# Two layers of a gated Flamingo-style network on one core: transposed q and k projections in the self attention, a later output product in the first cross attention, and phase ends without a second wait

## What is computed

```
x = x + tanh(g_xattn[0]) * _L0_xattn_ref(_layernorm(x), ctx_2048, ...)   # 16 heads of 128, keys 64 per sequence
x = x + tanh(g_ffn[0])  * _L0_ffn_ref(_layernorm(x), ...)                # self attention, then mixture of experts

q = (h @ wq + bq).reshape(b, s, H, HD).transpose(0, 2, 1, 3)             # H = 16, HD = 128
k = (h @ wk + bk) ...;  v = (h @ wv + bv) ...
q = q * cos + _rotate_half(q) * sin
k = k * cos + _rotate_half(k) * sin                                      # _rotate_half: (-x2, x1) of the halves of a head
probs = softmax(q k^T / sqrt(HD), causal);  out = (probs @ v) @ wo + bo
```

## Time and profile before

| | |
|---|---|
| median of 3 runs | 2107.55 us (2107.46 to 2110.78) |
| profiled execution: its time, its span | 2106.73 us, 2104.8 us |
| PE / PEld / DVE / ACT / POOL busy | 88% / 77% / 52% / 58% / 47% of the span |
| mean granted PE clock | 0.937 |
| x0, f0 in the trace | about 95 to 394 us, 448.6 to 1112 us |

### The profile page before, as it was taken

The page is one execution under the profiler, slowest core; times in us unless marked ns, Lnnn a source line. Parts: engine busy times, 40 slices in busy tenths (PEclk is TensorE's granted clock), DMA queues, the critical chain, the costliest instruction groups (busy, mean ns, idle before and its releaser), DMA issues.

```text
span 2104.8 us, 36109 instructions
## 1 busy us (share of the span) xinstructions
PE 1850.6 (88%) x11456; PEld 1614.3 (77%) x11456; DVE 1100.6 (52%) x3059; ACT 1228.7 (58%) x4061; POOL 979.7 (47%) x1133
## 2 busy tenths in 40 slices
PE   3599999449999999999997897489999999999698
PEld 1377887327888888888887785278888888988598
DVE  1467666555565565565552443455555555555422
ACT  1266777225666666666662331388888888888321
POOL 2333333276775775775543101254444444444255
PEclk9699999659999999999995898699999999999799
DMA  3000000100000000000000101000000000000000
GB/s 102 23 13 16 16 21 26 48 29 31 11 31 16 12 31 16 11 16 16 11 11 1 33 25 38 22 7 11 10 8 11 11 11 11 18 18 12 4 16 26
DMA packets 29069, 42.26 MB, mean 20 GB/s; under 512 B 4690, under 2 KB 18514, under 8 KB 28628
## 3 DMA queue, kind: packets, MB, share of 16 engines
q1 hardware_dynamic: 28884, 39.96, 6.3%
HBM read 35.76 MB, written 4.19 MB: 19 GB/s over the span
## 4 chain that ended last, share of the span: by engine, by line
PE 65%; ACT 13%; issue 6%; DVE 5%; POOL 3%; PEld 1%; DMA 1%; POOLq 1%; SPq 0%; PEldq 0%; DVEq 0%; ACTq 0%
PE pA L460 6%; PE pA L462 6%; PE pA L461 6%; PE pS L894 4%; PE pF L460 3%; ACT pA L1444 3%; PE pF L461 3%; PE pF L462 3%; PE pF L626 3%; PE pO L913 3%; PE pS L605 3%; PE pT L886 2%; ACT x_P L1470 2%; PE pT L903 2%; PE pO L1363 1%
## 5 line engine op out<-in xcount | busy, mean ns | idle before, releaser
L460 PE MATMUL pA<-Wh,XTh 128*128 128x512 f32 (+1 forms) x768 | 345.8, 450 | 21.9 <-POOLq L120 12.1
L462 PE MATMUL pA<-Wh,XTl 128*128 128x512 f32 (+1 forms) x768 | 292.9, 381 | 0.0
L461 PE MATMUL pA<-Wl,XTh 128*128 128x512 f32 (+1 forms) x768 | 292.0, 380 | 0.0
L455 POOL TENSOR_TENSOR Wl<-RAW,Wh 128x512 fp32r<-128x512 f32 (+3 forms) x96 | 102.1, 1063 | 402.0 <-ACT Wh L448 402.0
L460 PEld LDWEIGHTS pA<-Wh,XTh 128*128 128x128 f32 x768 | 148.6, 193 | 51.3 <-POOLq L120 13.3
L1192 POOL TENSOR_TENSOR f_t<-f_t,f_RB 128x512 f32<-128x512 f32 x128 | 165.3, 1291 | 16.9 <-DVE f_t L1076 16.7
L462 PEld LDWEIGHTS pA<-Wh,XTl 128*128 128x128 f32 x768 | 148.0, 193 | 28.8
L461 PEld LDWEIGHTS pA<-Wl,XTh 128*128 128x128 f32 x768 | 148.8, 194 | 26.6
L1076 DVE TENSOR_TENSOR f_t<-pA,f_sin 128x512 f32<-128x512 f32 x128 | 88.5, 692 | 140.7 <-PE pA L462 99.9
L1470 ACT ACTIVATE x_P<-x_P,x_nm 128x192 f32<-128x192 f32 (+1 forms) x256 | 127.3, 501 | 32.6 <-DVE x_nm L1579 32.5
L1002 ACT ACTIVATE f_P<-f_P,f_nm 128x128 f32<-128x128 f32 (+1 forms) x256 | 113.6, 447 | 49.7 <-DVE f_nm L1095 49.4
(11 more groups left out here) (247 smaller groups left out, 5873.1 us busy)
## 6 DMA issues: line engine op xcount, KB each, us to landing
RAW<-in_w_f SPq DMA_DIRECT2D x32, 256.0 KB, 2.6
RAW<-in_w_x SPq DMA_DIRECT2D x32, 160.0 KB, 2.2
RAW<-in_w_x SPq DMA_DIRECT2D x32, 128.0 KB, 2.0
RAW<-in_w_ff SPq DMA_DIRECT2D x8, 288.0 KB, 2.8
R<-in_x SPq DMA_DIRECT2D x4, 512.0 KB, 5.9
x_spill<-R SPq DMA_DIRECT2D x1, 2048.0 KB, 7.5
f_bqk<-in_f_b SPq DMA_DIRECT2D x4, 512.0 KB, 3.7
RAW<-in_w_moe SPq DMA_DIRECT2D x8, 256.0 KB, 2.7
```

The costliest lines, as they stand in the source:

```text
L455: pool.tensor_tensor(Wl[slot][:, at], RAW[:, s, 0:cw], Wh[slot][:, at].bitcast(F32), ALU.subtract).then_inc(split_done, 1)
L460: e.matmul(o, ah, bh, start=first, stop=False)
L461: e.matmul(o, ah, bl, start=False, stop=False)
L462: return e.matmul(o, al, bh, start=False, stop=last)
```

## The change

It has three parts.

**Phase ends.** All engines wait for `bar`; `cleared` is gone. POOL clears the old phase's semaphores behind that wait, while the others go on. The semaphores of a phase are given back one phase later than before, so neighbouring phases use different ones.

**x0.** `out_proj(i - 1)` stands behind `p_tr(i)` in PE's order, and the last one behind the loop. PT and VW get a second copy each; DVE's `add_out` follows one step later, inside the softmax.

**f0.** q and k are projected transposed: weights stationary, 256 tokens moving, twelve matrix multiplications of 128x256 for each n (two heads, two k tiles, three products). The parts are now n = 0: q of heads 0 and 1, n = 1: k of heads 0 and 1, n = 2 and 3 the same for heads 2 and 3. Since a head's features lie on partitions, its halves are swapped by ACT, `swapped`: two copies of 64x512 from pA to the other half of `sw`, which has two buffers. DVE `take` writes (pA + bias) x cos straight to qT or kT, two operations of 128x256. POOL `rotate` has three operations of 128x512: sw x sin, + RB, and the sum. `qk_tr` and `qk_ev` are gone. RB is made by ACT (`swapped_bias`, two operations of 128x256 in 12 of the steps and four times ahead of them). `w_high` and `w_low` are both on DVE. qT and kT get a second copy.

```
         def phase_end(e, name):
             k = phases.setdefault(name, len(phases) + 1)
             e.drain().then_inc(bar, 1)
+            e.wait_ge(bar, 5 * k)
             if e is nc.gpsimd:
-                e.wait_ge(bar, 5 * k)
                 for h in sems_of[name]:
                     e.sem_clear(h)
-                e.nop().then_inc(cleared, 1)
-            e.wait_ge(cleared, k)
...
                     p_tr(i)
-                    out_proj(i, s)
+                    if not first:
+                        out_proj(i - 1, 1 - s)
                 in_order(e, NI, body, 24)
+                out_proj(NI - 1, (NI - 1) % 2)
...
+                    if i >= 2:
+                        add_out(i - 2)
                     if two_more:
                         queries(i + 2, s, 0)
...
-                    for k in range(KD):
-                        cc = slice(w0 + k * GW, w0 + (k + 1) * GW)
-                        ins = three(e, pA[:, n % 2, :], x_part(XTh, i, k, t), x_part(XTl, i, k, t),
-                                    Wh[g % 2][:, cc], Wl[g % 2][:, cc], k == 0, k == KD - 1)
+                    for a in range(2):
+                        o = pA[:, n % 2, a * S:(a + 1) * S]
+                        h = 2 * (n // 2) + a
+                        for k in range(KD):
+                            at = WK * (n % 2) + k * GW + h * HD
+                            w = slice(at, at + HD)
+                            xh, xl = XTh[:, k, b], XTl[:, k, b]
+                            e.matmul(o, Wh[g % 2][:, w], xh, start=(k == 0), stop=False)
+                            e.matmul(o, Wh[g % 2][:, w], xl, start=False, stop=False)
+                            ins = e.matmul(o, Wl[g % 2][:, w], xh, start=False, stop=(k == KD - 1))
...
+                def swapped(i, n):
+                    m = NT * i + n
+                    e.wait_ge(q["proj"], NQ * i + n + 1)
+                    e.wait_ge(q["rope"], pos(m - 1))
+                    for r in range(2):
+                        src, dst = slice(r * H2, (r + 1) * H2), slice((1 - r) * H2, (2 - r) * H2)
+                        ins = e.activation(sw[dst, n % 2, :, :], pA[src, n % 2, :].rearrange("p (a n) -> p a n", a=2),
+                                           ACT.Copy)
+                    ins.then_inc(q["sw"], 1)
...
                     if n < 4:
+                        e.wait_ge(q["sw"], NT * i + n + 1)
+                        e.wait_ge(q["sc"], pos(HG * (i - 1)))
+                        x = (kT if n % 2 else qT)[:, i % 2, 2 * (n // 2):2 * (n // 2) + 2, :]
+                        for a in range(2):
+                            h = (i // 8) * HG + 2 * (n // 2) + a
+                            ins = e.scalar_tensor_tensor(x[:, a, :], pA[:, n % 2, a * S:(a + 1) * S],
+                                                         bqk[:, n % 2, h:h + 1], cosd[:, :], ALU.add, ALU.mult)
+                        ins.then_inc(q["taken"], 1)
...
                 def rotate(i, n):
                     m, g = NT * i + n, i // 8
+                    y = sw[:, n % 2, :, :]
+                    x = (kT if n % 2 else qT)[:, i % 2, 2 * (n // 2):2 * (n // 2) + 2, :]
+                    e.wait_ge(q["sw"], m + 1)
+                    e.tensor_tensor(y, y, bc(sind[:, :], 1, 2), ALU.mult).then_inc(q["swm"], 1)
+                    e.wait_ge(q["swm"], m + 1)
+                    e.wait_ge(q["rb"], 2 * NT * g + 2 * n + 2)
+                    e.tensor_tensor(y, y, RB[:, g % 2, 2 * n:2 * n + 2, :], ALU.add).then_inc(q["swb"], 1)
+                    e.wait_ge(q["swb"], m + 1)
                     e.wait_ge(q["taken"], NQ * i + n + 1)
                     e.tensor_tensor(x, x, y, ALU.add).then_inc(q["rope"], 1)
```

More of the change, by code:

```diff
@@ L774, in body @@
                     if last:
+                        add_out(i - 1)
                         add_out(i)
@@ L880, in qk_tr @@
[L880 to L888 removed]
+                    if n >= 4:
+                        for k in range(KD):
+                            cc = slice(WV + k * GW, WV + (k + 1) * GW)
+                            ins = three(e, pA[:, n % 2, :], x_part(XTh, i, k, n - 4), x_part(XTl, i, k, n - 4),
+                                        Wh[g % 2][:, cc], Wl[g % 2][:, cc], k == 0, k == KD - 1)
+                        ins.then_inc(q["proj"], 1)
+                        return
@@ L931, in pe @@
                     proj(0, n)
-                for n in range(NT):
-                    qk_tr(0, n)
                 proj(1, 0)
@@ L1016, in o_ev @@
                     e.activation(OTh[:, i % 2, h, :], pO[:, 0:S], ACT.Copy).then_inc(q["oth"], 1)
-                def w_high(i):
-                    g = i // 8
-                    e.wait_ge(q["proj"], NQ * 8 * g)
-                    e.wait_ge(q["f"], pos(i - 1))
-                    high_w(e, raw_in, q["hi"], cw_next if g == G - 1 else cw_here, i, i % 2, (g + 1) % 2)
+                e.wait_ge(q["const"], 64)
                 for n in range(NT):
-                    qk_ev(0, n)
+                    swapped_bias(0, n)
+                    swapped(0, n)
+                swapped(1, 0)
                 exp(0, 0)
+                swapped(1, 1)
                 normalise(0, 0)
+                swapped(1, 2)
                 exp(0, 1)
                 for i in range(NI):
-                    j = i + 1
-                    one = j < NI
+                    j, k = i + 1, i + 2
+                    one, two = j < NI, k < NI
                     p_ev(i, 0)
+                    if one:
+                        swapped(j, 3)
                     normalise(i, 1)
@@ L1142, in dve @@
                     recip(i, 3)
+                    w_high(i)
                     o_low(i, 1)
+                    w_low(i)
                     if i:
                         add_out(i - 1)
+                    if one:
+                        soft(j, 0)
                     if two:
@@ L1149, in dve @@
                     if one:
-                        soft(j, 0)
-                    if two:
-                        take(k, 1)
-                    if one:
                         recip(j, 0)
```

225 lines of the change are left out of this document (75 added, 150 removed).

## The result

The changed kernel takes 2048.65 us (median of 4 runs, 2046.52 to 2050.59), the kernel before in the same series 2109.16 (2107.46 to 2111.98). The ratio is 0.9712, with a 95% interval of 0.9695 to 0.9728: 60.5 us less, where 2057 us and 50.0 us less than the profiled run were forecast. The profiled execution has a span of 2046.1 us.

A forecast was written before the change was run, and what follows sets the result against it. PE was taken to bound f0, and after the change a loop through sw's two buffers. Gains 14.3 + 17.8 + 9.4 + 0.9 + 6.1 + 1.5 = 50.0 us off 2106.73 gave 2057 us; eight-in-ten range 2038 to 2088.

The forecast's parts named there:

- Phase ends: At all phase ends, 210 semaphore clears leave the path and 0.6 us come back in layer norms: 14.3 us gained.
- x0: First cross attention: PE's 0.69 us wait for the PT copy goes in 30 steps, less the last step's cost: 17.8 us.
- the likeliest case: The forecast itself, with an f0 period of 19.4 to 19.8 us and its unknown prices: chance 0.56, 2048 to 2068 us.
- The tail: End of x0: the last step pays for one more output product and addition, taken as 2.9 us lost.
- f0, what PE saves: Each f0 step loses 1.95 us of transposes, new projections cost nothing; PE alone would need 17.86 us a step.
- f0, the loop: Loop through sw's two buffers, rotations 0 and 1 and proj(k,5): period 19.6 us instead of 19.81, 6.1 us gained.
- The sign named beforehand: In f0, PE idle 1.5 to 1.8 us before each proj(·,5), released by DVE; a PE wait elsewhere would be wrong.
- f0, its start: f0 starts 9.4 us earlier, with small constants; first period gives 0.9 more, the stretch behind proj(31,5) 1.5.
- The unbound loop: Rival, chance 0.10: f0's loop does not bind, PE never waits before proj(k,5); period 17.9, 2008 us.
- ScalarE was not late: Rival, chance 0.17: ACT's swaps in f0 wait behind exp or softmax copies; period 20.0 to 20.6, 2069 to 2086 us.
- The collision of GpSimd and VectorE: Rival, chance 0.10: w_high and w_low on DVE hold up rotations 0 and 1; period 20.6 or 21.0, 2086 or 2098 us.
- The other rule that was weighed: Following copies overlap by about 93 ns: f0's loop 0.19 us shorter, sum 5.4 us lower; the forecast did not use it.

The follow-up runs named there:

- four buffers: The changed kernel with four buffers of sw instead of two, so the swap of n = 3 waits only for the step before's rotation: 2015.73 us, ratio 0.9552.
- both GpSimd experiments: The changed kernel with one more 128x512 GpSimd operation in rotations n = 0 and 1: 2168.77 us; or in n = 2 and 3: 2053.99 us.
- the split on the other engines: The changed kernel with the weights' high part back on ScalarE and low part on GpSimd, in places beside the loop: 2049.85 us, ratio 0.972.

## Why the prediction was right or wrong

The range and the direction were right, and so was the mechanism of f0. The time lies 8.4 us under the forecast value, at the lower edge of the likeliest case's own range (2048 to 2068). Against the 50.0 us of the forecast the traces differ by 58.7: 7.5 more in x0 and 3.2 more in f0's periods, 2.0 less in the rest.

- **Phase ends**: 14.3 forecast, 13.6 measured alone. That the clears lie beside other work except ahead of two norms was confirmed by clearing twice.
- **x0**: 17.8 forecast, 26.4 measured alone. This is the term that was mis-sized. It was "30 x 0.69 = 20.7 us", with the price taken from the idle time of the earlier trace rows; the runs show 0.90 to 0.93 a step, 28.1 us. The tail, 2.9, is 2.8 in the trace (28.1 less the 25.3 to the last addition). The surplus is outside the bound that the prediction gave this term (2 us more), and inside the range of the sum only because that was wide enough for it. The wait was gone as forecast; its price has to be read from start to start.
- **f0, what PE saves**: "PE alone would need 17.86 us": 17.87 with four buffers, when the two gaps that are left are taken out. The new projections cost nothing, as said. Of the 1.95 us that the transposes took, 0.3 was a wait: at 772.74 the four of KR start 0.74 us behind the four of QR, at 768.06 only 0.44. That wait went with them, so the sum holds. From `proj(j,5)` to the end of `proj(k,0)` it is 7.87 us instead of the 7.98 forecast.
- **f0, the loop**: 19.63 us forecast and 19.6 taken, 19.49 measured. Every link was found where it was put: swap 1.19 (1.21), two rotations 7.98 from 711.29 to 719.27 (8.04), swap 1.19, take 0.88. The four buffers and both GpSimd experiments show that it is this loop. The sign named beforehand, 1.5 to 1.8 us of idle PE before `proj(·,5)` and no wait elsewhere, came out only in part: 1.07 is printed, 1.31 from start to start, and 0.31 stands ahead of `proj(k,3)`. 29 periods gave 9.3 us instead of 6.1, since 0.1 us counts 29 times.
- **f0, its start**: 9.4 forecast, 8.7; first period 0.9 and 0.3; behind the last projection 1.5 and 2.4. In all 11.8 forecast, 11.4 measured.
- **The rivals.** The unbound loop would have needed more buffers. ScalarE was not late for the loop with two buffers (its swap of n = 1 kept `proj(k,3)` back by 0.31 us, beside the loop), but it is what remains with four. The collision of GpSimd and VectorE occurs, in the changed kernel at the other end: not POOL's rotations but DVE's copy is held up. The timeline and the view of that line show it:

```profile
706.56 1.42 DVE L1098 CAST Wh<-RAW 128x512 fp32r<-128x512 f32 x1
```
```profile
L1098 DVE CAST Wh<-RAW x32: 426/1419/1496, 455.4 to 1050.6; 128x512 fp32r<-128x512 f32 x32
```
```profile
706.40 1.28 POOL L1170 TENSOR_TENSOR f_kT<-f_kT,f_sw 128x512 f32<-128x512 f32 x1
```

The copy takes 0.43 us at least and 1.42 in the median, and here it ends 0.30 us after the POOL operation that began ahead of it. POOL's 384 operations of f0 stay between 1.26 and 1.30 us. It goes both ways, though, where the timing differs: with the operation added in n = 2 and 3, DVE's copy and the subtraction behind it (711.90 to 714.88) run beside the two POOL operations of 1.47 and 1.61 us shown above. By the rule in the Trainium skill, "SBUF — State Buffer", section "SBUF: two separate sides", who comes first keeps the shared port for a whole instruction and the other waits; the trace agrees. Its price for the loop was nothing, as the kernel with the split on the other engines shows. The other rule that was weighed, "ScalarE: Activation LUTs", section "What ACT_TABLE_LOAD costs" in the Trainium skill, would have made a swap pair 0.09 us shorter than two singles: the trace disagrees within a pair, with 1.19 us for two of 0.593. It agrees with the rule for what follows: the normalising behind the swap of 719.37 starts at 720.47, 0.09 before that swap ends, which shortens nothing in the loop.

What stays open: why the second cross attention starts later than in the kernel before, by 1.4 us in the changed kernel and by 0.6 to 3.2 in the kernels with one part alone. The trace of the changed kernel shows one DMA issue of 1.48 us ahead of it instead of 0.43, in a stretch in which the instruction queue has a packet that the kernel before lacks. That alone is not the cause: with the phase ends alone no issue there is long, and the start comes 2.0 us later all the same.

## What to carry to other kernels

Price a wait on TensorE by the distance between starts, with and without it, not by the idle time that a view prints: here 0.93 against 0.69 us, and gaps of 0.3 us with no idle time at all. When a change takes work off the bounding engine, look for the loop through buffers that it leaves, and add up its links; two buffers in such a loop can give back nearly all that was saved (of 1.95 us a step off TensorE, 1.62 came back as waiting). Where several engines work in strict order around a single buffer, moving one operation ahead moves the wait to the buffer's other reader; reorder all who share it, or add a buffer.

## What was not expected of the hardware

- A loop that leaves TensorE waiting can lose clock on top. In the kernel with an added operation in n = 0 and 1 the period was 21.9 us at a granted clock of 1.00 and 23.5 when it fell to 0.93, with 2.9 us of idle time ahead of `proj(·,5)` in each step of either kind; with 1.07 us (the changed kernel) the clock stayed at 1.00.
- The last 36 products of the program ran at 0.72 of the clock after a wait of 3.28 us, and at 1.00 after the same wait in the kernel before (windows of both):

```profile
2095.70:2100.20 4.50, 4.37 (x36) 4.17 (x36) 0.00 (x0) 0.00 (x0) 0.04 (x1) 1.00 0.14 46
```
```profile
2035.40:2041.50 6.10, 5.98 (x36) 5.78 (x36) 0.00 (x0) 0.00 (x0) 0.03 (x1) 0.72 0.11 36
```

  That is the 1.4 us which the last phase is longer, but it can't be put down to the change: nine more traces of this study, those of each part alone among them, have the same 0.72 behind the same wait, and only that of the kernel before has 1.00. Why that one kept its clock is open.
